# Eight more dummy matmuls in each MLP group of a one-layer vision tower with slot experts

## The reference, cut to what matters

```
h = tokens(x)                                   # (16, 36, 192)
h = h + attention(layernorm(h))
xn     = rms_norm(layernorm(h)) * norm_weight
logits = slots_normalised @ normalised(xn)      # (16, 64 slots, 36 tokens)
dispatch = softmax over tokens, combine = softmax over slots
y = dispatch-weighted sum of xn                 # (16, 64, 192)
y = gelu(y @ fc1_weight[s] + fc1_bias[s])       # 64 x (192 x 768)
y = y @ fc2_weight[s] + fc2_bias[s]             # 64 x (768 x 192)
out = h + combine-weighted sum of y
```

## Time and profile before

| What | Value |
|---|---|
| Median of three runs | 229.45 us |
| All runs | 230.4, 229.45, 226.4 us |
| The profiled execution's own time | 230.38 us |
| Its span, first to last instruction | 228.6 us |
| Mean granted TensorE clock | 0.963 |
| TensorE (PE) busy | 198.1 us, 87% |
| VectorE / ScalarE / GpSimd busy | 29% / 27% / 20% |
| DMA, mean over the span | 353 GB/s, 80.68 MB |

### The profile page before, as it was taken

One profiled execution on the slowest core, in us unless ns is written; L12 is line 12 of the kernel. 1 busy time (PEld: TensorE's weight loads), 2 busy tenths in 40 slices (PEclk: granted clock), 3 DMA queues, 4 the chain that ended last, 5 costly groups with the idle time before them and its releaser, 6 DMA issues.

```text
span 228.6 us, 4769 instructions
## 1 busy us (share of the span) xinstructions
PE 198.1 (87%) x2026; PEld 128.2 (56%) x2026; DVE 65.5 (29%) x153; ACT 62.5 (27%) x161; POOL 45.7 (20%) x91
## 2 busy tenths in 40 slices
PE   6499989999888999879969969969969969956994
PEld 6399856667667737437427527527517616711562
DVE  1655463659856453011011012002002002000203
ACT  2351423355535445131131041041041031021100
POOL 7800168556536131001001001001001000000000
PEclk9889999999999999999999999999999997997589
DMA  6999999318999979999999999999999999999602
GB/s 167 264 232 421 412 412 380 71 40 284 424 415 414 422 276 419 402 425 422 410 411 419 423 414 411 420 419 418 409 422 422 409 412 420 421 411 411 254 2 77
DMA packets 18371, 80.68 MB, mean 353 GB/s; under 512 B 2665, under 2 KB 5806, under 8 KB 14062
## 3 DMA queue, kind: packets, MB, share of 16 engines
q1 hardware_dynamic: 18350, 80.38, 90.1%
HBM read 79.46 MB, written 0.91 MB: 352 GB/s over the span
## 4 chain that ended last, share of the span: by engine, by line
PE 67%; DMA 15%; DVE 8%; ACT 5%; issue 3%; POOL 0%; DVEq 0%
PE ps L1253 15%; PE ps L1278 14%; DMA ring<-in_L_ffn_fc_weight_dram 12%; PE ps L1230 7%; PE ps L888 5%; ACT x_space L625 4%; PE ps L1220 4%; PE ps L1264 3%; PE ps L882 3%; DMA ring<-in_x_dram 3%; PE ps L1003 2%; PE ps L975 2%; PE ps L957 2%; PE ps L1112 2%; PE ps L914 2%
## 5 line engine op out<-in xcount | busy, mean ns | idle before, releaser
L1253 PE MATMUL ps<-ring,qkvT 128*32 128x384 f32 x384 | 42.6, 577 | 2.8 <-DMA ring<-in_L_ffn_fc_weight_dram 2.4
L859 DVE TENSOR_TENSOR region_p<-ps,b1T 128x384 f32<-128x384 f32 x16 | 8.8, 557 | 107.5 <-PE ps L1264 107.5
L1278 PE MATMUL ps<-ring,x_space 128*32 128x192 f32 x768 | 37.9, 351 | 1.1 <-issue 1.1
L1278 PEld LDWEIGHTS ps<-ring,x_space 128*32 128x32 f32 x768 | 26.9, 116 | 11.8 <-issue 6.9
L625 ACT ACTIVATE x_space<-ps,row_scale 128x384 f32<-128x384 f32 x16 | 14.7, 917 | 37.3 <-PE ps L1253 37.3
L1253 PEld LDWEIGHTS ps<-ring,qkvT 128*32 128x32 f32 x384 | 11.2, 112 | 22.4 <-issue 18.8
L1264 PE MATMUL ps<-ident,x_space 128*128 128x128 f32 x48 | 9.0, 301 | 14.5 <-ACT x_space L625 14.5
L1264 PEld LDWEIGHTS ps<-ident,x_space 128*128 128x128 f32 x48 | 5.2, 145 | 27.1 <-ACT x_space L625 26.9
L442 POOL COPY bias_space<-ident 64x128 f32<-64x128 f32 x8 | 2.2, 285 | 86.0 <-PE ps L1220 86.0
L1230 PE MATMUL ps<-projT,soft_space 128*108 128x192 f32 (+1 forms) x96 | 18.6, 336 | 0.4 <-ACT projT L656 0.4
L656 ACT COPY projT<-ps 128x192 f32<-128x192 f32 x8 | 2.5, 319 | 55.9 <-PE ps L1278 55.9
(11 more groups left out here) (139 smaller groups left out, 223.6 us busy)
## 6 DMA issues: line engine op xcount, KB each, us to landing
ring<-in_L_ffn_fc_weight_dram SPq DMA_DIRECT2D x32, 2304.0 KB, 24.2
ring<-in_x_dram SPq DMA_DIRECT2D x2, 864.0 KB, 8.5
ring<-in_L_tok_W_proj_dram SPq DMA_DIRECT2D x1, 576.0 KB, 7.8
ring<-in_L_attn_w_qkv_dram SPq DMA_DIRECT2D x1, 432.0 KB, 11.0
out_dram<-h SPq DMA_DIRECT2D x2, 162.0 KB
value_store<-ring SPq DMA_DIRECT2D x1, 258.2 KB
ring<-value_store SPq DMA_DIRECT2D x3, 86.1 KB
ring<-value_store SPq DMA_DIRECT2D x3, 66.9 KB
```

Source lines behind the costliest of these rows:

```text
L859: dve.tensor_tensor(pre[:, pr, :, :].rearrange("p c (k b) -> p c k b", b=B), ps[:, 2 + pr, 0:384].rearrange("p (c k b) -> p c k b", c=3, b=B),
L1253: mm = pe.matmul(ps[32 * k:32 * k + 32, pr, 0:FF // 2], y_group[:, g % 2, j, 2 * pr + qq, :], w[:, qq, j, :, 3 * hf:3 * hf + 3], start=(j ...
L1278: mm = pe.matmul(ps[32 * q:32 * q + 32, 4, 0:D], gact[:, q // 2, k, 32 * l:32 * l + 32], w[:, q, c, :], start=(l == 0 and c == 0), stop=(l ...
```

## The change

Two calls of `keep_busy` are added. From group 1 on, five dummy matmuls stand between `turn_hidden(g, 0)` and `first_layer(g, 1)`, and three between `combine(g - 1, ...)` and `second_layer(g, 1)`. Group 0 gets none, group 7 gets both. Nothing else changes; all of them write bank 3.

```diff
@@ -1286,6 +1286,7 @@
                     spread_sums()
                 else:
                     turn_hidden(g, 0)
+                    keep_busy(3, 5)
                 first_layer(g, 1)
                 if g == 0:
                     turn_combine()
@@ -1301,6 +1302,7 @@
                 second_layer(g, 0)
                 if g:
                     combine(g - 1, 1 - g % 2)
+                    keep_busy(3, 3)
                 second_layer(g, 1)
                 if 0 < g < GROUPS - 1:
                     keep_busy(3, 5)
```

## The result

The changed kernel takes **239.89 us** in the median of four runs (236.94 to 241.28); the kernel before, in the runs shared with it, 228.88 us (226.4 to 230.4). The ratio is 1.044 with a 95% interval of [1.024, 1.065]: slower, as forecast, and 2.9 us above the predicted 237.0. The ratio is taken from the runs without a long drop of the clock only, here 236.94 and 239.28 us; both lie in the forecast range of 234.2 to 239.8, and the median of all four lies 0.1 us above it. The profiled execution took 239.28 us with a span of 237.5.

A forecast was written before the change was run, and what follows sets the result against it. TensorE's chain was taken as the bound until unit 29: span 228.60 + 14.67 dummies - 2.49 slack - 1.67 and - 3.87 half clock = 235.24, and with 1.78 own time 237.0 us; range 234.2 to 239.8.

The forecast's parts named there:

- What bounds the kernel: MLP until unit 29: TensorE's own work is the chain, with a slack of only about 2.5 us against DMA.
- The slack: Added TensorE work before unit 29 that DMA's bound hides: 2.49 us, or 4.16 us with the dip gone.
- The price of the dummies: Groups 1 to 7: 56 dummies at 0.262 us each, paid in full, 14.67 us.
- The seams: Joins at the two new places, 13 or 14 in all: -1.0 to +2.5 us, taken as zero.
- What hides them: At both new places TensorE has no idle to absorb dummies; the following ScalarE wait moves along, so full price.
- No transfer late again: Unit 31's load issues by 185.1 us and lands by 218.1; TensorE wants it near 227.
- The sum without dips: Whole kernel at full clock in the MLP: span 235.25 us plus 1.78 own time, 237.0 us.
- The clock: Half-clock stretches at 190.7 us and in group 7 go away, saving 1.67 and 3.87 us.
- one or more dips stay: Rival: half clock stays at 190.7, 238.7 us, or also in group 7, 242.6 us; chance 20%.
- four equal groups: Groups 2 to 5 stayed at clock 1.00; reason for counting the 1.67 us stretch at 190.7 as gone.
- Cheap dummies: Rival: dummies in the new places cost 0.16 us each, 8.96 us in all, giving 231.3 us; chance 5%.
- DMA as the bound: Rival: TensorE has room and unit 29 is still waited for at 206.81, giving 227.4 us; chance 5%.

The follow-up runs named there:

- Half loads: Units 9 to 31 load only half their weights: kernel before 222.95 us at a clock of 1.000, changed kernel 237.06 and 238.34 us at 0.993.
- two per group: Kernel before plus two dummies between turn_hidden(g, 0) and first_layer(g, 1), 14 in all: ratio 0.999 [0.994, 1.004].
- no dummies: Kernel before without the five dummies per group behind second_layer in groups 1 to 6: ratio 0.995 [0.990, 1.000], lowest 226.4 us.
- the busiest kernel: Changed kernel plus three dummies in each of a group's two ScalarE waits: 238.09 us in the median of four, ratio 1.042 [1.032, 1.051].
- only five: Changed kernel without the three dummies between combine and second_layer: profiled execution 230.94 us, three others 233.68 to 240.06.
- only three: Changed kernel without the five dummies between turn_hidden and first_layer: ratio 1.010 [1.003, 1.017], profiled execution 230.41 us.
- group 7 only: Kernel before plus the change's five and three dummies in group 7 alone: ratio 1.002 [0.996, 1.008], median 228.39 us.
- half loads after: Changed kernel with units 9 to 31 loading only half their weights: 237.06 and 238.34 us at a clock of 0.993, two others 246.05 and 246.89.
- the second wait filled: Changed kernel plus three dummies in the second ScalarE wait of a group only: 244.04 us in one execution.
- the first alone: Changed kernel plus three dummies in the first ScalarE wait of a group only: 239.22 us in one execution.

## Why the prediction was right, and its size a little low

**What bounds the kernel: right.** Until unit 29 the chain is TensorE's own work, with a small slack against DMA. Half loads, two per group and no dummies show it from three sides. The slack was forecast at 4.16 us without dips of the clock, and is 3.5 to 4.7 in the runs (226.42 to 227.6 against 222.95).

**The price of the dummies: right, 5% high.** 14.67 us forecast, 13.9 in the trace and 14.1 from the half loads. The seams were bounded at -1.0 to +2.5; they came out at -0.8. The first dummy behind the transposes starts 0.38 us after them, 0.10 earlier than `first_layer` did (0.48), and the five take 1.21 us up to line 1253 (178.20 - 176.99), not 1.31. The group of three costs 0.07 to 0.08 more than 3 x 0.262.

**What hides them: right.** Nothing in the chosen places. The same number in ScalarE's wait costs 0.03 us a group.

**No transfer late again: right.** Not one wait for a unit; the last one lands at about 217 us, 20 us before the end.

**The sum without dips: right, and its closeness luck.** 237.0 forecast, 236.94 in the run at full clock. But the profiled execution less its two stretches is 239.28 - 1.68 - 1.57 = 236.0 us, since the dummies cost 0.8 less than forecast and group 1 starts 0.24 earlier. Where group 1 starts varies between executions (93.19 to 94.53 us in nine traces, all with a granted clock near 1.00 ahead of it), so an agreement to 0.1 us is chance.

**The clock: the term that was mis-sized.** I credited 1.67 + 3.87 us for half-clock stretches that would go, and gave their staying 20%. Only one of four runs had a full clock (mean 1.000, 0.976, 0.971, 0.962: 236.94, 239.28, 240.5, 241.28 us); where the clock fell in the last two no trace shows. In the profiled one the stretches cost 1.68 + 1.57 us. Against the forecast's working: group 1 starts 0.24 earlier, six groups at 19.40 and 1.68 for the stretch give unit 28 at 211.76 (measured 211.75, forecast 211.03). So it is off by only 0.7 because the dummies priced 0.7 too high and the earlier start took back part of the stretch that it left out. The case "one or more dips stay" should have been the likeliest, with about 239. The argument used against it, that four equal groups had stayed at 1.00, rested on one execution: of 58 runs of the kernel before in three sessions only one had a mean clock of 1.000, and eight traces of kernels with both ScalarE waits open have 13 stretches, 1.6 per execution.

**The rivals.** Cheap dummies are out: line 882's 172 records in the loop have the median of the earlier trace rows, 275 ns, and five in the new place take 1.21 us, 121 ns per record. The Trainium skill, "TensorE: Matmul & The Clock Gate", "Back-to-back issue gap", with its 81 ns per N=128 matmul doesn't fit these float32 dummies, which take 131 ns per record at the old place. DMA as the bound is out. Part 1 of the same page of the Trainium skill, that activity releases the throttle, isn't contradicted, but the busiest kernel still had a run at 0.964, and even at 1.000 the changed kernel is 9.3 us slower.

**What stays open** is what brings the half clock in the MLP. In the eight profiles with both ScalarE waits open (before, after, only five, only three, none, two per group, group 7 only, half loads after), 13 stretches begin on the first line 1278 of a group, behind two waits for ScalarE, the transposes and line 1220 (one of them, in the kernel with the change in group 7 only, also behind waits for units), and none elsewhere in the loop unless a wait for a unit came first. With the second wait filled, alone or with the first (four profiles), there was none; with the first alone, one. That points to the second wait, but in 43 of 56 groups none begins there with it open, and one profile per kernel isn't proof. No variant with full loads beat the kernel before beyond the noise: at best it takes 226.4 us, as the kernel without dummies does, and only halving the bytes brought it lower (222.95).

## What to carry to other kernels

Ask of a dummy or any added instruction what its engine would have done at that moment. In a wait it is free (0.03 us for eight here); in a stretch that is the chain it is paid in full (1.98 us for the same eight), once the slack against the other bound is used up. When two resources look full, the waits tell which one sets the time, and the first wait that appears late in the run shows how much slack is left (2.49 us here, and 4.16 without the stretch ahead of it). Clock dips of one profiled execution are a draw: count them over several runs before crediting their end to a change.

## What was not expected of the hardware

The half-clock stretches of the MLP start almost always on the same line, behind idle of no more than 1.04 us at a time. At half clock the 48 records of line 1278 take 3.84 us against 2.16, while the following line 1230 is at full speed again. And filling every wait of the MLP with matmuls (group 19.42 us, TensorE idle 0.2 us at a time) did not hold the mean clock at 1.000 in three of four runs. Where it fell in these three isn't known; it can lie ahead of the MLP, as in the trace with only the second wait filled, where group 1 started 8 us late.
